# A decoder layer on one core: self-attention scores of all 16 heads in one pass over eight small TensorE tiles, the causal mask put in by the same small tiles

## The reference

```python
def _L0_attn_ref(x, W_qkv, W_out):
    qkv = jnp.einsum('bsd,ed->bse', x, W_qkv)
    ...
    Q, K, V = (qkv[0], qkv[1], qkv[2])
    scores = jnp.einsum('bhqd,bhkd->bhqk', Q, K) / jnp.sqrt(jnp.float32(D_K))
    causal_mask = jnp.triu(jnp.ones((seq_len, seq_len), dtype=bool), k=1)
    scores = jnp.where(causal_mask, jnp.float32(-jnp.inf), scores)
    attn = jax.nn.softmax(scores, axis=-1)
    out = jnp.einsum('bhqk,bhkd->bhqd', attn, V)
    ...
x = x + _L0_attn_ref(_layernorm(x, axis=-1), L0_attn_W_qkv, L0_attn_W_out)
x = x + _L0_xattn_ref(_layernorm(x, axis=-1), ctx_2048, mask_BxS2_bk0)
x = x + _L0_ffn_ref(_layernorm(x, axis=-1), ...)
```

## Time and profile before

| | us |
|---|---|
| median of 3 runs | 256.02 (255.43 to 256.05) |
| span of the profiled execution | 255.1 |
| PE busy / PEld busy | 218.9 / 166.9 |
| DVE busy | 215.7 |
| ACT busy / POOL busy | 147.8 / 110.4 |

### The profile page before, as it was taken

How to read it: one execution, slowest core, us unless ns; L and a number is a source line. 1 busy time by engine, 2 the same in 40 slices (tenths; PEclk the granted TensorE clock), 3 DMA queues, 4 the chain that set the end, 5 groups by cost and what they waited for, 6 DMA issues and landing times. The chain is left out here.

```text
span 255.1 us, 7444 instructions
## 1 busy us (share of the span) xinstructions
PE 218.9 (86%) x2384; PEld 166.9 (65%) x2384; DVE 215.7 (85%) x639; ACT 147.8 (58%) x386; POOL 110.4 (43%) x209
## 2 busy tenths in 40 slices
PE   3867899989899999999999999999999999666433
PEld 3646686757686868686868686868687877442211
DVE  1398948699999998999899989998999999988751
ACT  2024273656685858585858585858585858443131
POOL 7212011337272626272726272727263626464540
PEclk9975999999999999999999999999999999985555
DMA  6992001010101010101010101001010101000000
GB/s 227 370 356 83 0 3 42 4 41 3 45 22 44 23 42 21 41 21 41 21 41 21 41 21 40 21 25 37 7 54 6 57 27 40 0 23 1 21 22 21
DMA packets 11090, 12.59 MB, mean 49 GB/s; under 512 B 1024, under 2 KB 10304, under 8 KB 11072
## 3 DMA queue, kind: packets, MB, share of 16 engines
q1 hardware_dynamic: 11008, 12.36, 14.8%
q0 software_dynamic: 64, 0.00, 0.0%
HBM read 10.26 MB, written 2.10 MB: 48 GB/s over the span
## 5 line engine op out<-in xcount | busy, mean ns | idle before, releaser
L1356 POOL TENSOR_TENSOR zh<-hh,gd 128x352 f32<-128x352 f32 x16 | 15.2, 947 | 55.0 <-DVE hh L1033 55.0
L328 PE MATMUL bankU<-yaT,wqkv 128*128 128x128 f32 x256 | 35.0, 294 | 0.8 <-ACT yaT L635 0.6
L328 PEld LDWEIGHTS bankU<-yaT,wqkv 128*128 128x128 f32 x256 | 32.5, 206 | 3.0 <-ACT yaT L635 1.6
L1332 POOL TENSOR_SCALAR ve<-mv 128x1 f32<-128x1 f32 x48 | 9.8, 205 | 51.0 <-DVE mv L875 30.5
L1334 POOL TENSOR_TENSOR rs<-ve,neghalf 128x1 f32<-128x1 f32 x48 | 26.5, 552 | 4.0
L312 PE MATMUL psS<-kz,qT 32*64 32x128 f32 x512 | 21.3, 280 | 0.0
L301 PE MATMUL bankG<-wg,zT 128*128 128x352 bf16 x64 | 15.9, 331 | 5.4 <-DVE hh L1033 3.6
L635 ACT ACTIVATE pT<-psS 128x512 f32<-128x512 f32 x32 | 19.1, 596 | 0.9
L1378 POOL TENSOR_SCALAR hq<-zh,qh 128x704 f32<-128x704 f32 x16 | 13.7, 857 | 11.6 <-issue 10.2
L340 PE MATMUL bankA<-wqkv,yaT 128*64 128x128 f32 x256 | 18.4, 288 | 0.0
L407 PE MATMUL bankB<-wo,oT 128*128 128x256 f32 x64 | 16.7, 384 | 1.7 <-ACT oT L635 1.5
(11 more groups left out here) (125 smaller groups left out, 583.9 us busy)
## 6 DMA issues: line engine op xcount, KB each, us to landing
ct_in<-ctx_t SPq DMA_DIRECT2D x16, 128.0 KB, 2.0
cn_in<-ctx_n SPq DMA_DIRECT2D x16, 128.0 KB, 2.1
out<-o_out SPq DMA_DIRECT2D x16, 128.0 KB, 1.7
wg<-gate_t SPq DMA_DIRECT2D x1, 1408.0 KB, 9.2
x_in<-x SPq DMA_DIRECT2D x1, 1280.0 KB, 11.6
wqkv<-wqkv_t SPq DMA_DIRECT2D x1, 768.0 KB, 6.1
wd<-down_t SPq DMA_DIRECT2D x1, 640.0 KB, 9.0
x_in<-x SPq DMA_DIRECT2D x1, 512.0 KB, 8.6
```

Of the source, the lines that this page charges most:

```text
L328: last = pe.matmul(qk_ps[:, e * P:(e + 1) * P], wqk[:, c, e * P:(e + 1) * P], yaT[:, c, :], start=(c == 0), stop=(c == DC - 1))
L1356: G.tensor_tensor(zh[:, 0:HALF], hh[:, 0:HALF], gd[:, 0:HALF], ALU.mult).then_inc(ev["zh_d0"], 1)
```

## The change

All 16 heads' scores are made in one call in place of two. The call stands where `scores_0` stood; `scores_1` is gone from the lists. It has 16 mask matmuls (32x64 tiles, 256 columns, bf16) in place of four full ones, and 16 score matmuls, as before eight and eight, now over four row groups in turn. The mask is made by row group g as two products: `pick_bf` (which of the 64 queries a partition stands for) times the mask rows of these queries, first queries 0 to 31, then 32 to 63. The two signals `s_ps0` and `s_ps1` become one, `s_ps`, which comes with the last matmul. The array of constants grows from 514 to 898 columns.

```diff
-C_ID, C_CAUSAL, C_PARITY, C_SEQ = 0, 128, 384, 386
-C_ALL = 514
+C_ID, C_CAUSAL, C_PICK, C_PARITY, C_SEQ = 0, 128, 640, 768, 770
+C_ALL = 898
...
-            def score_group(st, half):
-                for g in (2 * half, 2 * half + 1):
-                    pe.matmul(psS[:, g, 0:256], ident_bf[:, :], causal_bf[:, :], start=True, stop=False)
+            def score_groups(st):
+                for half in range(2):
+                    for g in range(4):
+                        rows = slice(32 * g, 32 * g + 32)
+                        for b in range(2):
+                            pe.matmul(psS[SEQ * b:SEQ * (b + 1), g, 0:256], pick_bf[rows, half, :],
+                                      causal_bf[rows, half, :], start=(half == 0), stop=False)
                 for c in range(DC):
-                    for g in (2 * half, 2 * half + 1):
+                    for g in range(4):
                         rows = slice(32 * g, 32 * g + 32)
                         for b in range(2):
                             last = pe.matmul(psS[SEQ * b:SEQ * (b + 1), g, c * P:(c + 1) * P],
                                              qT[rows, c, SEQ * b:SEQ * (b + 1)],
                                              kz[rows, c, b, :, :], start=False, stop=(c == DC - 1))
-                last.then_inc(ev[f"s_ps{half}"], 1)
+                last.then_inc(ev["s_ps"], 1)
...
                 if st.has(0):
-                    scores_0(st, ([], [(0, "pT_d0"), (0, "sub_d0")]))
+                    scores_all(st, ([], [(0, "pT_d0"), (0, "sub_d0")]), ([(0, "pT_d1")], [(0, "sub_d1")]))
...
-                if st.has(0):
-                    scores_1(st, ([(0, "pT_d1")], [(0, "sub_d1")]))
...
             def maxima_0(st):
-                dve.wait_ge(ev["s_ps0"], st.n(dve, 1))
+                dve.wait_ge(ev["s_ps"], st.n(dve, 1))
...
             def maxima_1(st):
-                dve.wait_ge(ev["s_ps1"], st.n(dve, 1))
+                dve.wait_ge(ev["s_ps"], st.n(dve, 1))
...
-            V.tensor_copy(causal_bf[:, :], cst[:, C_CAUSAL:C_CAUSAL + 4 * SEQ]).then_inc(cst_bf, 1)
+            V.tensor_copy(pick_bf[:, :, :].rearrange("p h q -> p (h q)"), cst[:, C_PICK:C_PICK + 2 * SEQ])
+            V.tensor_copy(causal_bf[:, :, :].rearrange("p h n -> p (h n)"), cst[:, C_CAUSAL:C_CAUSAL + 8 * SEQ]).then_inc(cst_bf, 1)
```

More of the change, by code:

```diff
@@ L116, in decoder_kernel @@
         ident_bf = sb("ident_bf", [P, P], BF16)
-        causal_bf = sb("causal_bf", [P, 4 * SEQ], BF16)
+        causal_bf = sb("causal_bf", [P, 2, 4 * SEQ], BF16)
+        pick_bf = sb("pick_bf", [P, 2, SEQ], BF16)
         seq_bf = sb("seq_bf", [2, P], BF16)
@@ L220, in decoder_kernel @@
         wmean_set = sem("wmean_set")
-        names = ("st1_d var1 ve1_d rstd1 ya_d yaT_ps yaT_d qk_ps q_d k0_d k1_d v_ps v_d s_ps0 s_ps1 mx_d0 mx_d1 "
+        names = ("st1_d var1 ve1_d rstd1 ya_d yaT_ps yaT_d qk_ps q_d k0_d k1_d v_ps v_d s_ps mx_d0 mx_d1 "
                  "sub_d0 sub_d1 exp_d0 exp_d1 pT_ps0 pT_ps1 pT_d0 pT_d1 o_ps_d rsum_d oN_d oT_ps oT_d y_ps x1_d "
@@ L343, in project_v, with scores_all @@
                 last.then_inc(ev["v_ps"], 1)
-            def scores_0(st, users):
+            def scores_all(st, users, users2):
                 pe.wait_ge(ev["q_d"], st.n(pe, 1))
@@ L350, in scores_0 @@
                 freed(pe, st, users)
[L351 to L359, removed]
+                freed(pe, st, users2)
+                score_groups(st)
             def transpose_weights_0(st, users):
@@ L644, in keep_q @@
                 act.wait_ge(ev["qk_ps"], st.n(act, 1))
-                after(act, ev["s_ps0"], st.n(act, 0))
-                after(act, ev["s_ps1"], st.n(act, 0))
+                after(act, ev["s_ps"], st.n(act, 0))
                 copy(qT[:, :, :].rearrange("p c t -> p (c t)"), qk_ps[:, 0:D]).then_inc(ev["q_d"], 1)
@@ L1475 @@
     const[:, C_ID:C_ID + P] = np.eye(P)
-    const[:, C_CAUSAL:C_CAUSAL + 4 * SEQ] = np.where(np.arange(4 * SEQ)[None, :] % SEQ > r[:, None] % SEQ, -BIG, 0.0)
+    for half in range(2):
+        query = r % 32 + 32 * half
+        const[:, C_CAUSAL + 4 * SEQ * half:C_CAUSAL + 4 * SEQ * (half + 1)] = np.where(
+            np.arange(4 * SEQ)[None, :] % SEQ > query[:, None], -BIG, 0.0)
+        const[:, C_PICK + SEQ * half:C_PICK + SEQ * (half + 1)] = np.arange(SEQ)[None, :] == query[:, None]
     for j in range(2):
```

## The result

The change made the kernel slower by a little: 256.91 us (255.92 to 259.32, 18 runs) against 256.05 (255.41 to 258.94, 18 runs of before beside them), a ratio of 1.0053 with a 95% interval of 1.0031 to 1.0075. The forecast was 255.9 and no change. The time lies within the range of 253.4 to 257.1, but it is a loss clear of the noise: 0.86 us between the medians, 1.4 us (0.8 to 1.9) by the ratio, which need not be that of the medians. The ratios are taken from fast runs alone, while the medians and ranges here are of all runs, with three slow ones (259.10 to 259.96 us) among the twelve of the reordered kernel with large constants, and one run of 627.12 us of the last kernel left out.

A forecast was written before the change was run, and what follows sets the result against it. Neither PE nor DVE alone was taken as the limit: PE reaches the second gate-up half as DVE finishes `hh`. Span 255.1 + 0.5 - 0.6 + 0.0 x 12 = 255.0, median 0.9 above: 255.9 us, range 253.4 to 257.1.

The forecast's parts named there:

- The steady step: In 12 steady steps, 0.9 us saved on PE becomes waiting for `hh` ahead of L301; gain 0.
- The hinge at the first `hh`: The second gate-up half (L301) starts 0.15 us after `hh` ends on DVE in all 16 tiles, so DVE sets it.
- the period that the prediction built from two pieces: Step without turn: DVE from cross maxima to `hh`, 6.04 us, plus PE from L301 to cross scores, about 6.9.
- The grown group: The single group of 16 mask and 32 score instructions on PE grows by +0.05 us (0 to 0.1).
- the pair price of 26 to 32 ns: Slower rival, fixed price per small load and matmul: 256.7 us at 26 ns (0.08), 258.7 at 32 (0.07 from 28).
- Fill: PE's saving of some 0.8 us in step 2 arrives in fill: gain 0.6 us, bounds 0 and 0.65.
- the named wait: DVE's 0.53 us wait for the cross scores in step 3 of fill, forecast to be gone.
- Start: 197 KB more constants load ahead of `wqkv` and `wg`, so `wg` lands later: +0.5 us, bounds 0.3 and 0.7.
- The cast: One longer and one new DVE cast, an estimated 0.4 us, fall into DVE's 4.33 us wait for `wg`.
- the term 0.0 x 12: The loop's part of the sum: no change in each of 12 steady steps.
- The clock: Slower rival: full clock returns only behind tile 1's scores, PE's work at 26 to 30 us longer; 257.0 us, chance 0.05.
- the faster rival: DVE's 0.4 us steady wait for the cross scores goes in six steps, 2.4 us, giving 253.5 us; chance 0.13.

The follow-up runs named there:

- the reordered kernel with large constants: The changed kernel, constants and two casts kept, with `transpose_weights_0` moved ahead of `gate_up_1` in the steady steps: 256.53 us, ratio 1.0002.
- the last kernel: Small constants, one cast, `transpose_weights_0` moved, `ya` transposes in bank G, plus ScalarE's `keep_hT_0` ahead of `squares_0`: 253.78 us, ratio 0.9913.
- Six matmuls put back: Kernel with small constants and one cast, plus six unread matmuls (0.64 us) ahead of the transposes of `hb` each steady step: 255.22 us, ratio 0.997.
- the reordered list: Kernel with small constants and one cast, with `transpose_weights_0` moved ahead of `gate_up_1` in the steady steps: 255.4 us, ratio 0.9968.
- small constants and one cast: The changed kernel with the mask kept once for 64 keys and repeated by access pattern, constants again 514 columns: 255.27 us, ratio 0.9963.
- The kernel with one cast: The changed kernel with picks and mask in one tile filled by one cast, large constants kept: 256.64 us, ratio 1.0014.
- both the move and bank G: Small constants and one cast, `transpose_weights_0` ahead of `gate_up_1`, transposes of `ya` written to bank G in place of bank U: 254.26 us, ratio 0.9937.

## Why the prediction was right and wrong

**The steady step: right for PE's time.** Zero gain from it was forecast, and the steps without a turn have 13.00 us in both kernels. PE's saving turned into a wait for `hh` of 0.81 us, forecast 0.9, and the cross scores were waited for as before. Six matmuls put back for nothing confirm it. What the sum put at nothing in the loop and was not nothing is the cast, below.

**Its reason: half right.** The hinge at the first `hh` is there. That PE then "works without a gap that another engine ends until the cross scores end" is wrong: 3.0 us behind the start of L301 (133.19 to 136.17) it waits for the second `hh`. The wait was all but closed in before, where PE without it comes only 0.04 us sooner. The sum was not hurt, since both hinges hold PE back, but the period that the prediction built from two pieces (6.04 on VectorE, 6.9 on PE) was put together wrongly. It would have forecast 2.3 us for the reordered list, which brought none. The prediction took the constant 0.15 us behind the first `hh` for a hinge in all 16 tiles, and did not look for the same constant elsewhere.

**The grown group: right, at its low end.** Forecast +0.05 us, measured 1.05 against 1.04 when taken to the matmul on `px` in both kernels. The row of four score matmuls was the right one to go by, and the pair price of 26 to 32 ns wrong. The single starts in after bear out the rounds of eight: at 127.185 to 127.208 eight matmuls begin some 3 ns apart, and the next rounds begin at 127.318, .427, .536, .645 and .755, 0.11 us apart. The loads show it too:

```profile
127.18 0.16 PEld L311 LDWEIGHTS psS<-causal_bf,pick_bf 32*64 32x64 bf16 x16
127.32 0.53 PEld L317 LDWEIGHTS psS<-kz,qT 32*64 32x64 f32 x32
```

32 loads in 0.53 us are 17 ns each. The rule that the prediction weighed (the Trainium skill, "TensorE: Matmul & The Clock Gate", section "Wait — 56ns, not 53.3ns?": no two starts less than some 25 ns apart) does not hold for these tiles: by it 32 starts would span 0.8 us, and the 32 score matmuls took 0.66 us from the first start to the last end (L317 above).

**Fill: the sign right, the named wait wrong.** The wait did not go:

```profile
47.60 0.29 DVE L1011 TENSOR_SCALAR zb<-zq 128x256 bf16<-128x256 f32 x1 [0.69 <-POOL zq L1342]
...
48.55 0.29 DVE L932 TENSOR_REDUCE nmx<-bankA 128x1 f32<-128x128 f32 x1 [0.48 <-PE bankA L420]
```

Against the earlier trace rows `zb` stands where it did if counted from the landing of `wg` (36.52 us in both), and the cross maxima 0.95 us behind it, before 1.18. PE came 0.23 sooner there, not 0.8. By the first `hh` of that step the gain is 0.4. Which instruction of PE in step 2 gave the rest back was not settled. The 0.4 is that of one pair of profiles: against the four profiles of the list of before, the seven of the changed list without a second stretch at half clock gain 0.2 to 0.9, in the mean 0.6, so the size forecast is not refuted; the three with that stretch are 0.4 to 1.4 us behind all four.

**Start: the sign right, the size not refuted.** The working, bytes by 382 GB/s, gave 0.51; the landing of `wg` moved by 0.4 to 1.1, by how the two groups are compared, 0.7 between their lowest values. Its own scatter, over 1 us from one execution to the next, leaves it there.

**The cast: the step that failed.** The prediction put one longer and one new cast at an estimated 0.4 us of VectorE time that falls "into that 4.33 us wait". That is true of their time and was not the cost. The new instruction stands ahead of VectorE's loop, and the entry and four turns became 0.8 us longer by the rows of waits, 0.6 by the positions of `hh`, and so in all three profiles with four casts. In the sum the loop is the term 0.0 x 12, where it measured +0.6. No case of the prediction had this; the list of "instructions that it issues" was costed by their duration alone.

**The sum.** Forecast: +0.5 - 0.6 = -0.1. By the terms as they came: start +0.7 (0.4 to 1.1), loop +0.6, fill -0.4 (-0.2 to -0.9), in all +0.9. Between the medians +0.86 was measured, but +1.4 (0.8 to 1.9) by the ratio, so the agreement with the median is partly luck. For small constants and one cast the terms give -0.4, and it is -0.6 between the medians and -0.95 (0.5 to 1.4 of gain) by the ratio. So up to half a microsecond is unexplained in both; the scatter of fill, of the drain (over 1 us) and of the start is large enough for it, but nothing ties it to one of them. The prediction's own range is a slip, too: its bounds for start and fill give 255.6 to 256.7, not 255.3 to 256.8.

**The clock: a rival left open.** Where TensorE's clock fell during fill differs from one execution to the next, whatever the kernel: at half from 15.9 to 26.1 us in the profile of before, from 18.3 to 25.1 in that of after. In neither is it low past 28 us, which the prediction named as a sign against itself. The profile of the kernel with one cast has a second stretch, from 31.2 to 34.6 us:

```profile
PEclk9997979999999999999999999999999999965555
```

It puts the first `hh` of step 3 at 43.0 us behind the landing of `wg`, in place of 41.7 in after, 1.4 us of price. The profiles with six more matmuls and with both the move and bank G have it too, so it is not tied to the large constants; the run with six more took 256.57 us, where eight of the ten took 254.8 to 255.3. All three have the changed list, and none of the four profiles with the list of before has one that late, which is too few to tell. After also has more long runs: with its constants and casts, reordered or not, 10 of 30 runs lie above 258 us, against 3 of 106 of before, 2 of 24 with the large constants in two other kernels, and none of 55 of the six kernels with the changed list and small constants, which are faster by up to 2.2 us (the kernel with twelve more matmuls and the run of 627 us are not counted). No profile fell on such a run of after. So it is open whether a clock at half, and with it this rival, makes up part of the 1.4 us.

**The rivals for a gain and for a pair price did not come.** What the faster rival spoke of, VectorE's wait for the cross scores, could be had by half, but by the order of the lists and a bank together, not by PE's time alone. The loop gained 1.3 us, where that rival had 2.4 with step 15.

## What to carry to other kernels

A start that follows an end on another engine by the same interval in every step is a wait, even if the profile shows no idle time ahead of it; look for all of them before a chain is called free, since time saved between two such hinges is worth nothing until the second is moved. Cost a change by its data too: here the matmuls were free, and 197 KB in front of the first needed weights together with one cast ahead of the loop made the difference between 0.4% faster and 0.5% slower. Line two kernels up on an early event before their spans are compared, and look at the turn of a loop whenever an instruction is added ahead of it.

## What the runs showed of the hardware

- The first VectorE instruction behind a loop's turn started 82 to 84 ns after the start of the last register instruction in kernels with three casts ahead of the loop, and 201 to 212 ns in those with four; at the entry 102 and 466 ns. The loop took 0.6 us more for it.
- At both hinges the matmul that waited for `hh` started 0.145 to 0.148 us behind its end in before and after, for the first `hh` in all 16 tiles, for the second in ten of twelve steps.
- 32 loads and matmuls of 32x64 tiles spread over all eight places of the array (four row groups, two column halves) took as long as 16 over four places: 0.66 us for 32 and 0.67 for 16, from the first start to the last end. Eight of them began 3 ns apart, the next eight 0.11 us behind.
- With 197 KB more ahead of it, a load of 1408 KB landed 0.7 us later, lowest against lowest (10.30 and 10.99 us), where the size over the measured rate gives 0.51; with the same bytes its landing scattered by 1.6 us (10.30 to 11.88).
- With the clock at half from 20.9 to 24.3 and again from 31.2 to 34.6 us, in place of 18.3 to 25.1 alone, fill up to the first `hh` of step 3 took 1.4 us more (43.03 against 41.67 us).
